# Four token passes instead of one and three in the gate and up projections of a sandwich block on eight cores

## What is computed

```python
def _L0_ffn_ref(x, w_gate, w_up, w_down):          # weights are int32
    gate = jnp.einsum('bsd,hd->bsh', x, w_gate * SCALE)      # 1024 -> 3072
    up   = jnp.einsum('bsd,hd->bsh', x, w_up * SCALE)        # 1024 -> 3072
    h = jax.nn.silu(gate) * up
    return jnp.einsum('bsh,dh->bsd', h, w_down * SCALE)      # 3072 -> 1024

x = x + _layernorm(attn(_layernorm(x)))            # x: (4, 4096, 1024) float32
x = x + _layernorm(ffn(_layernorm(x)))
```

## Time and profile before

| | |
|---|---|
| median of 2 runs | 1436.31 us (1435.57 to 1437.06) |
| the profiled execution | 1433.69 us |
| its slowest core, 6 | span 1432.1 us |
| spans of the eight cores | 1412.8 to 1432.1 us |
| TensorE busy on core 6 | 1213.3 us, 85% of the span |
| DMA queue of POOL | 41.95 MB, 25.2% of 16 engines' span |

### The profile page before, as it was taken

The page is one execution under the profiler, slowest core; times in us unless marked ns, Lnnn a source line. Parts: engine busy times, 40 slices in busy tenths (PEclk is TensorE's granted clock), DMA queues, the critical chain, the costliest instruction groups (busy, mean ns, idle before and its releaser), DMA issues.

```text
span 1432.1 us, 14493 instructions; the slowest of 8 cores (1412.8 to 1432.1 us)
## 1 busy us (share of the span) xinstructions
PE 1213.3 (85%) x5274; PEld 519.2 (36%) x5274; DVE 376.0 (26%) x608; ACT 216.5 (15%) x337; POOL 117.0 (8%) x140
## 2 busy tenths in 40 slices
PE   0798887779999999999994166566899999999997
PEld 0233332223444444444441022222344444444443
DVE  2243334301111211111122342334221121224343
ACT  0111111210221221122121001111111111100000
POOL 0011110000000000000000022222111212000000
PEclk9999999999999999999997577777899999999999
DMA  9755566651232232233224999999748586423422
GB/s 184 154 117 138 138 146 144 139 106 30 59 74 45 52 68 59 44 67 66 45 52 113 202 150 158 168 151 136 103 48 100 49 99 82 52 89 88 117 90 88
DMA packets 280309, 143.59 MB, mean 100 GB/s; under 512 B 254640, under 2 KB 254640, under 8 KB 280240
## 3 DMA queue, kind: packets, MB, share of 16 engines
q0 software_dynamic: 107664, 41.95, 25.2%
q1 hardware_dynamic: 102688, 79.74, 21.7%
q10 hardware_dynamic: 69888, 20.98, 7.3%
HBM read 117.48 MB, written 25.17 MB: 100 GB/s over the span
## 4 chain that ended last, share of the span: by engine, by line
PE 78%; DMA 14%; DVE 3%; issue 2%; ACT 1%; POOL 1%; ACTq 1%; SPq 0%; DVEq 0%; POOLq 0%
PE ps_pv L650 16%; PE ps_q L543 16%; PE ps_g L954 12%; PE ps_d L1116 12%; PE ps_u L966 11%; PE ps_s L256 7%; DMA wu_sb<-wuT 6%; DMA xnT_sb<-xn_bf 4%; PE ps_e L305 3%; DMA xn2T<-xn_bf 1%; PE ps_s L252 1%; DMA xs<-x 1%; PE ps_pv L427 1%; POOL wg_sb L931 1%; DMA s_FM<-s_tok 1%
## 5 line engine op out<-in xcount | busy, mean ns | idle before, releaser
L954 PE MATMUL ps_g<-xn2T,wg_sb 128*128 128x512 bf16 x768 | 205.7, 416 | 116.9 <-DMA wu_sb<-wuT 62.6
L543 PE MATMUL ps_q<-s_FM,ebuf 128*128 128x512 bf16 x1024 | 225.5, 381 | 8.6 <-DMA ebuf<-e_sc 8.6
L650 PE MATMUL ps_pv<-s_tok,PT_sb 128*128 128x512 bf16 x1024 | 225.3, 381 | 0.9 <-DVE g_bc L493 0.9
L966 PE MATMUL ps_u<-xn2T,wu_sb 128*128 128x512 bf16 x768 | 194.8, 399 | 0.0
L1116 PE MATMUL ps_d<-wdT_sb,h_act 128*128 128x512 bf16 x768 | 165.9, 379 | 1.0 <-DVE h_act L989 1.0
L954 PEld LDWEIGHTS ps_g<-xn2T,wg_sb 128*128 128x128 bf16 x768 | 78.4, 104 | 225.5 <-issue 149.5
L543 PEld LDWEIGHTS ps_q<-s_FM,ebuf 128*128 128x128 bf16 x1024 | 100.3, 98 | 131.2 <-issue 12.3
L650 PEld LDWEIGHTS ps_pv<-s_tok,PT_sb 128*128 128x128 bf16 x1024 | 100.4, 98 | 123.2 <-issue 3.4
L989 DVE SCALAR_TENSOR_TENSOR h_act<-silu_b,ps_u 128x512 bf16<-128x512 f32 x96 | 65.9, 687 | 293.6 <-PE ps_u L966 293.6
L256 PE MATMUL ps_s<-wspT_sb,xnT_sb 128*128 128x512 bf16 x512 | 137.1, 416 | 0.0
L966 PEld LDWEIGHTS ps_u<-xn2T,wu_sb 128*128 128x128 bf16 x768 | 79.4, 103 | 105.2 <-issue 25.5
(11 more groups left out here) (67 smaller groups left out, 455.6 us busy)
## 6 DMA issues: line engine op xcount, KB each, us to landing
xs<-x SPq DMA_DIRECT2D x24, 1024.0 KB, 6.6
wg_sb<-wgT POOLq DMA_DIRECT2D x48, 256.0 KB, 5.1
wu_sb<-wuT POOLq DMA_DIRECT2D x48, 256.0 KB, 6.5
x_sc<-x_buf SPq DMA_DIRECT2D x16, 512.0 KB, 6.0
xs<-x_sc SPq DMA_DIRECT2D x16, 512.0 KB, 4.3
out<-out_b SPq DMA_DIRECT2D x16, 512.0 KB, 5.1
wdT_sb<-wdT POOLq DMA_DIRECT2D x4, 1536.0 KB, 13.6
e_sc<-e_stage POOLq DMA_DIRECT2D x32, 128.0 KB, 2.4
```

What stands on the lines that cost most here:

```text
L543: i = t.matmul(ps_q[:, slot, half * 512:(half + 1) * 512], ebuf[:, qt % 2, j, :], s_FM[:, j, qi * 1024 + half * 512: qi * 1024 + (half + 1 ...
L650: i = t.matmul(ps_pv2[:, nb * 512:(nb + 1) * 512], PT_sb[:, par, cb * P:(cb + 1) * P], s_tok[:, cb, nb * 512:(nb + 1) * 512], start=(cb == ...
L954: i = t.matmul(ps_g[:, slot, :], wg_sb[:, par, j, :], xn2T[:, j, tb * 512:(tb + 1) * 512], start=(j == 0), stop=(j == KC - 1))
L966: i = t.matmul(ps_u[:, slot, :], wu_sb[:, par, j, :], xn2T[:, j, tb * 512:(tb + 1) * 512], start=(j == 0), stop=(j == KC - 1))
```

## The change

Stage three runs four passes of one token block each instead of one pass of one block and one pass of three. Pass p goes over all 24 hidden blocks for `tb` = p. k now runs from 0 to 95, so `ffn_wload` is called 96 times instead of 48. The 12 LayerNorm tiles that were all in the first pass are spread: pass p (0, 1, 2) does tiles 4(p+1) to 4(p+1)+3 after blocks 1, 5, 9 and 13, and their normalisation and transposes after block 17. The four parts of `wdT_sb` are issued in pass 3, after blocks 0, 6, 12 and 18. The groups, their tiles and the number of matmuls stay the same.

```diff
-        l2n = 4
-        for hb in range(HC):
-            ffn_group(hb, hb, 0, hb % 4, hb % 4,
-                      w4=(rec[("xtr4", 0)] if hb == 0 else None))
-            if hb + 2 < HC:
-                ffn_wload(hb + 2)
-            if hb % 2 == 1 and l2n < NT_OWN:
-                l2_grpA(l2n)
-                l2n += 1
-            if hb in (10, 18):
-                g = (hb - 2) // 8
-                l2_sqrt(g)
-                l2_grpB(g)
-        l2_sqrt(3)
-        l2_grpB(3)
...
-        ffn_wload(HC)
-        ffn_wload(HC + 1)
-        wdT_part(0)
-        for hb in range(HC):
-            k = HC + hb
-            for tb in (1, 2, 3):
-                ffn_group(k, hb, tb, tb, tb,
-                          w4=(rec[("xtr4", tb)] if hb == 0 else None))
-            if k + 2 < 2 * HC:
-                ffn_wload(k + 2)
-            if hb == 6:
-                wdT_part(1)
-            if hb == 12:
-                wdT_part(2)
-            if hb == 18:
-                wdT_part(3)
...
+        for p in range(4):
+            if p == 3:
...
+            for hb in range(HC):
+                k = p * HC + hb
+                ffn_group(k, hb, p, hb % 4, hb % 4,
+                          w4=(rec[("xtr4", p)] if hb == 0 else None))
+                if k + 2 < 4 * HC:
+                    ffn_wload(k + 2)
+                if p < 3:
+                    if hb in (1, 5, 9, 13):
+                        l2_grpA(4 * (p + 1) + (hb - 1) // 4)
+                    if hb == 17:
+                        l2_sqrt(p + 1)
+                        l2_grpB(p + 1)
+                else:
+                    if hb in (0, 6, 12, 18):
+                        wdT_part(hb // 6)
```

More of the change, by code:

```diff
@@ L1016, in build_program @@
-        s_flush()
[L1018 to L1043, removed]
@@ L1062, in build_program, with wdT_part, f @@
[L1062 to L1065, removed]
+        wdT_sb = None
+        for p in range(4):
+            if p == 3:
+                s_flush()
+                l2_done = dict(sv=rec[("xn2", NT_OWN - 1)],
+                               ss=rec[("sq3g", NT_OWN // 4 - 1)],
+                               dt0=dtm[0].n, dt1=dtm[1].n,
+                               da0=da[0].n, da1=da[1].n,
+                               tr=[(s_, s_.n) for s_ in (dtp[0], dtp[1])])
+                ctx2.close()
+                wdT_sb = ctx34.enter_context(
+                    nc.sbuf_tensor("wdT_sb", [P, HC, D], BF16, side="right"))
+                def wdT_part(i4):
+                    def f(gp, i4=i4):
+                        if i4 == 0:
+                            gp.wait_ge(sv.h, l2_done["sv"])
+                            gp.wait_ge(ss.h, l2_done["ss"])
+                            gp.wait_ge(dtm[0].h, l2_done["dt0"])
+                            gp.wait_ge(dtm[1].h, l2_done["dt1"])
+                            gp.wait_ge(da[0].h, l2_done["da0"])
+                            gp.wait_ge(da[1].h, l2_done["da1"])
+                            for s_, v_ in l2_done["tr"]:
+                                gp.wait_ge(s_.h, v_)
+                        gp.dma_start(out=wdT_sb[:, i4 * 6:(i4 + 1) * 6, :],
+                                     in_=wdT_r[:, i4 * 6:(i4 + 1) * 6, :]
+                                     ).then_inc(dwF.h, 16)
+                    block.gpsimd(f)
+                    dwF.n += 16
+            for hb in range(HC):
[13 more added lines that the diff above has]
+                        wdT_part(hb // 6)
@@ L1066, in build_program @@
+        s_flush()
+        hmul_done = rec[("hmul", 4 * HC - 1, 3)]
+        ffn_done = dict(st=rec[("up_mm", 4 * HC - 1, 3)],
+                        ss=rec[("silu", 4 * HC - 1, 3)], sv=hmul_done)
         ctx23.close()
```

## The result

The changed kernel takes 1678.48 us (median), the kernel before 1439.77 us in the runs beside it. The ratio is 1.167, with a 95% interval of 1.164 to 1.170. Both medians include disturbed executions, which the ratio leaves out.

What follows compares the result with a forecast made beforehand. The prediction took the first pass as bound by weight loading, the second by TensorE. Stage three: 624 + 25 + 34 = 683 us against 439.8, giving 1680 us, range 1620 to 1735.

Steps and rivals of the forecast that it cites:

- Pass one as the pattern for all four: Stage three: all 96 groups run as in the old first pass, one per weight load, clock below 0.85.
- The quiet pair: Two successive groups with little LayerNorm traffic under way, in stage three: taken as 13.0 us for the slowest core.
- the first term: Stage three's weight loading over four passes: 48 pairs x 13.0 = 624 us, bounds 538 and 721.
- The LayerNorm: LayerNorm work of 12 tiles spread over three passes: costs 25 us in all, bounds 10 and 48.
- The down weights: Four down-weight transfers in pass 3 delay the weight loads behind them: 4 x 8.5 = 34 us, bounds 27 and 54.
- four gaps of 8 us or more: Sign in pass 3: TensorE gaps of that size behind L1039, showing the cost of the down weights.
- The sum: Whole of stage three up to the down projection: 683 us against 439.8, +243 us, kernel at 1680 us.
- Rival A: Stage three: DMA engines set the pace, even fast groups, 11.2 us a pair, 1593 us; chance 0.12.
- Rival B: Stage three: the old first pass's pace throughout, 15.0 us a pair, 1751 us; chance 0.15.
- Rival C: Stage three: not slower, since `wu_sb` loads get short; needs a landing of 2.8 us; chance 0.02.

## Why the prediction was right, step by step

**Pass one as the pattern for all four: right.** The loads are 96, the clock on core 3 is 0.77 to 0.79 (up to 0.87 in pass 2 of other cores, where I had said under 0.85), TensorE waits 238 us for `wu_sb` against some 230 forecast, and TensorE's busy time is up by 76 us (1289.1 against 1213.3) against some 95. I had taken 36 more slow groups; there are 31 (46 over 5 us on core 3, 15 on core 6 before). In passes 1 to 3 no core waits for transposes or for a slot of `ps_u`, as forecast.

**The quiet pair, 13.0 us: right.** Passes 1 and 2 without LayerNorm work have 13.0. The links were tested apart: half the bytes and one issue less bring 9.7, a fast clock 11.9, four places 8.9. That the figure was chosen between 12.6 and 15.0 "for the slowest core" is in part luck; the mean of the four pairs read, 12.6, would have given 605 us for the first term.

**The LayerNorm, 25 us in all: right as a sum.** By means of the cores and against a quiet pass of 156 us it is 11 + 13 + 2 = 26 us. The same sum in the kernel with one part of the down weights is 15 us, and with all the work in pass 0 it is 19, so 25 is right within what one execution tells. That nearly all of it lies with the chunk reads I had not said.

**The down weights, 34 us: somewhat too high.** Pass 3 is 182 - 156 = 26 us over a quiet pass, 6.5 a part, just under my lower bound of 6.7. Leaving three parts out gave 6.9 each. It is the term of the sum that was mis-sized. Of the sign "four gaps of 8 us or more", three cores show all four; core 3 has 5.7, 9.2, 7.9 and 7.9 us, and on every core the gaps at blocks 9, 15 and 21 are among the four longest of the pass.

**The sum.** Forecast were 624 + 25 + 34 = 683 us. Core 3, the slowest, took 688.1, and the mean of the cores is 677. Core 3 lies a little over the quiet pair of 13.0 (its pass 2 had 13.6 a pair, LayerNorm writes and transposes included). It also began the stage at 811.7 us, where core 6 began at 817.3 in the profile before, and the two differences cancel. That the sum met the median within 2 us is partly this luck. A slip in the working: the range was said to reach half-way into A and B. Half-way from 1680 would be 1637 and 1716; 1620 and 1735 are further out. The result lies inside either.

**Rival A was wrong in its limit.** I took 11.2 us a pair as what the DMA engines can do at best, from a share of 0.52 and 0.55. With four places they did a pair in 8.9. The step that failed is that a busy share of 1 means full. It made the lower bound of the first term (538 us) not a bound: 478 us was reached for the whole stage with the same transfers and more places. The 624 us of the forecast don't use it, but the 34 us of the down weights do: 8.5 us is a part's busy time, and "only 1.8 us of slack" is counted from 11.2.

**Rival B fell** with the kernel whose passes 1 and 2 are quiet (157 and 155 us, not 180). **Rival C** needed a landing of 2.8 us; in the changed kernel the shortest is 4.6 and the median 6.6. But there is a second way to C which I had not seen: not a shorter landing, but more loads in flight. It brings the kernel with four passes to within 4% of the kernel before, and still not below it.

## What to carry to other kernels

When a loop order is changed, count the compute that stands behind each load, and read the price of the new ratio from a stretch of the old trace that already has it; here pass one told the price of all four. A chain of "buffer free, issue, landing, compute" gets shorter with each of its links, and of the edits tried here more places brought the most, so ask first how many loads are in flight before calling a transfer-bound loop bound by bandwidth. With two places and one group per load, the gap also costs the clock (0.77 here), and the slow group is then a link of the chain that sets the next pair.

## What the runs showed of the hardware

**The mean busy share of the DMA engines is not bounded by 1 and doesn't tell that they are full.** At 0.91 core 3 of the changed kernel moved a load in 6.8 us, at 1.45 core 5 of the kernel with four places in 4.4, and on all eight cores the time was 6.3 to 6.8 and 4.4 to 4.6 us.

**Landing time and rate are two things.** With four places the median landing of `wu_sb` in pass 2 was 11.3 us against 6.3, while the rate rose by half.

**Reads of 1.5 MB from SyncE's queue slow POOL's weight loads; writes of 512 KB and transposes hardly do.** Taking four such reads away gave back 18 us by the ratio, and 26 or 14 us by the means of passes 0 and 1, by which execution it is compared with: 3.5 to 6.6 us a read.
